# Reordered engine queues and a mix over two 64-row halves in a cross-attention, attention and gated-MLP kernel

## What is computed

```
x = x + xattn(layernorm(x), ctx)        # 16 heads of 32, 1601 context rows per batch, latent width 32
x = x + attn(layernorm(x))              # 32 query heads of 128, 8 key/value heads, 512 selected keys + 64 new ones
x = x + ffn(layernorm(x))               # silu(x W1) * (x W3) W2, inner width 1792
# W = base + mean(|w - base|) * sign(w - base) for each of W1, W2, W3
```

## Time and profile before

| | us |
|---|---|
| median of 3 runs (lowest, highest) | 922.68 (922.39, 923.87) |
| profiled execution, its own time | 919.89 |
| its span in the trace | 917.8 |
| PE busy in the span | 851.7 |
| cross-attention (trace, until the barrier) | to about 288 |
| attention with keys | about 288 to 796 |
| MLP | from about 796 |

### The profile page before, as it was taken

One profiled execution on the slowest core, in us unless ns is written; L12 is line 12 of the kernel. 1 busy time (PEld: TensorE's weight loads), 2 busy tenths in 40 slices (PEclk: granted clock), 3 DMA queues, 4 the chain that ended last, 5 costly groups with the idle time before them and its releaser, 6 DMA issues.

```text
span 917.8 us, 15508 instructions
## 1 busy us (share of the span) xinstructions
PE 851.7 (93%) x5338; PEld 650.9 (71%) x5338; DVE 603.3 (66%) x993; ACT 519.1 (57%) x1005; POOL 459.6 (50%) x294
## 2 busy tenths in 40 slices
PE   6898899888987889999999999999999999899998
PEld 4455455544433668888788887887878878788886
DVE  5965567555625268578486684776848759768884
ACT  5655546555554466386474774655746657555552
POOL 2698788786751054544444444345454454154430
PEclk9899999999999999999999999999999999999999
DMA  8654244104103515032050230501505002535531
GB/s 359 217 199 153 99 153 171 28 19 136 58 1 121 193 43 207 24 134 97 0 206 23 95 133 0 206 23 41 187 0 203 15 0 92 184 127 194 192 107 46
DMA packets 42338, 102.96 MB, mean 112 GB/s; under 512 B 7858, under 2 KB 12978, under 8 KB 41394
## 3 DMA queue, kind: packets, MB, share of 16 engines
q1 hardware_dynamic: 42002, 102.06, 31.7%
q10 hardware_dynamic: 288, 0.26, 0.1%
HBM read 96.95 MB, written 1.05 MB: 107 GB/s over the span
## 4 chain that ended last, share of the span: by engine, by line
PE 51%; POOL 5%; DVE 3%; issue 3%; ACT 2%; DMA 0%; SPq 0%; DVEq 0%; POOLq 0%; ACTq 0%
PE psum L1401 9%; PE psum L1382 9%; PE psum L1517 8%; PE psum L1413 5%; PE psum L1531 4%; POOL w_piece L1908 3%; PE psum L1440 3%; PE psum L1431 3%; PE psum L1455 3%; PE psum L1436 3%; ACT w_piece L1624 2%; PE psum L1422 1%; PE psum L1432 1%; PE psum L1434 1%; DVE probs_t_low L1742 1%
## 5 line engine op out<-in xcount | busy, mean ns | idle before, releaser
L1896 POOL TENSOR_TENSOR head_probs<-head_probs,inverse_den 128x576 f32<-128x576 f32 x128 | 147.5, 1153 | 203.7 <-DVE inverse_den L1749 203.7
L1003 DVE TENSOR_REDUCE max_part<-psum 128x1 f32<-128x804 f32 x128 | 121.2, 991 | 38.4 <-PE psum L698 38.0
L901 ACT ACTIVATE probs<-psum 128x512 f32<-128x512 f32 (+1 forms) x208 | 106.7, 608 | 47.4 <-PE psum L719 46.4
L1631 ACT ACTIVATE head_probs<-psum,neg_max 128x576 f32<-128x576 f32 x128 | 94.7, 740 | 46.2 <-DVE neg_max L1766 45.8
L1766 DVE TENSOR_REDUCE neg_max<-psum 128x1 f32<-128x576 f32 x128 | 96.9, 757 | 23.8 <-PE psum L1401 21.3
L567 POOL TENSOR_TENSOR prob_sums<-prob_sums,probs 128x1024 f32<-128x1024 f32 (+1 forms) x42 | 100.2, 2386 | 18.4 <-ACT probs L901 14.1
L1742 DVE TENSOR_TENSOR probs_t_low<-psum,probs_t_high 128x512 fp32r<-128x512 f32 x124 | 84.8, 684 | 16.6 <-ACT probs_t_high L1637 15.6
L1413 PE MATMUL psum<-ident,head_probs 128*128 128x128 f32 x496 | 78.7, 274 | 16.5 <-DVE probs_t_low L1742 15.1
L719 PE MATMUL psum<-q_t,c_t 97*128 97x512 f32 (+1 forms) x208 | 76.1, 445 | 14.2 <-ACT q_t L919 7.1
L1401 PE MATMUL psum<-k_high,query_t_high 128*128 (+1 forms) x256 | 86.5, 338 | 1.9 <-DVE query_t_low L1721 1.4
L567 POOL TENSOR_TENSOR prob_sums<-probs 128x1024 f32<-128x1024 f32 x30 | 71.3, 2380 | 23.9 <-ACT probs L901 23.8
(11 more groups left out here) (227 smaller groups left out, 1948.2 us busy)
## 6 DMA issues: line engine op xcount, KB each, us to landing
ctx_t_odd<-in_ctx_dram SPq DMA_DIRECT2D x4, 3202.0 KB, 11.0
ffn_raw<-in_L_ffn_w_dram SPq DMA_DIRECT2D x42, 256.0 KB, 3.9
ffn_raw<-in_L_ffn_mean_w_dram SPq DMA_DIRECT2D x42, 256.0 KB, 4.1
w_piece<-in_L_ffn_w_dram SPq DMA_DIRECT2D x21, 512.0 KB, 6.5
w_piece<-in_L_ffn_mean_w_dram SPq DMA_DIRECT2D x21, 512.0 KB, 7.5
cache<-in_ctx_dram SPq DMA_DIRECT2D x3, 3202.0 KB, 10.8
wq_nat<-in_L_attn_wq_dram SPq DMA_DIRECT2D x32, 256.0 KB, 7.4
wo_nat<-in_L_attn_wo_dram SPq DMA_DIRECT2D x32, 256.0 KB, 3.2
```

The lines of the kernel that those rows point to most:

```text
L901: act.activation(prob_buffer(b, t)[0:rows, half * BANK:(half + 1) * BANK], psum[0:rows, n % SCORE_BANKS, :], ACT.Exp, scale=XSCALE).then_i ...
L1003: dve.tensor_reduce(max_part[:, qt, pair:pair + 1], psum[:, bank:bank + 2, 0:PIECE_KEYS], AX.XY, ALU.max).then_inc(s_max, 1)
L1631: act.activation(probs[:, qt, :].rearrange("p (a k) -> p a k", a=2), psum[:, 2 * (qt % 2):2 * (qt % 2) + 2, 0:HALF], ACT.Exp, bias=neg_max ...
L1896: pool.tensor_tensor(probs[:, qt, :], probs[:, qt, :], rden[:, qt:qt + 1].to_broadcast([P, KEYS]), ALU.mult).then_inc(s["norm"], 1)
```

## The change

Nine edits, no change to what is computed:

- `mix`: the 64 rows of `u` and the 64 of denominators are no longer stacked. `u_all` is one copy of the whole bank of 128 partitions (L1025), `d_all` another (L926). The products take 64 contraction rows (half 0 rows 0 to 63, half 1 rows 64 to 127): 16 with 32 columns against `wv_u`, then 16 with one column against `den_of`.
- `wv_u` and `den_of` are set up by five small memsets and four transfers in place of three memsets and two transfers.
- `shift_row` copies two halves of 512; the turned maxima signal after four transposes and after eight; each half of the first scores waits for its half.
- `max_scores` 5 to 14 each stand one place earlier in PE's list, ahead of `values` where they stood behind it.
- For the batches 5, 6 and 7, `copy_den` follows the batch's exponentials; for 5 and 6 `tail_and_denominators` goes ahead of `turn_max`.
- ACT: `abs_sum` ahead of `output_weight_high(g, 0)`.
- DVE: `values_low` ahead of `add_output` of tile 0.

```diff
-    u_all = core.sb("u_all", [P, 2, BANK], ctx=own)
+    u_all = core.sb("u_all", [P, BANK], ctx=own)
+    d_all = core.sb("d_all", [P, BANK], ctx=own)
...
-            sp.wait_ge(s_zero, 2)
-            for base in (0, LKV):
-                sp.dma_start(wv_u[base:base + LKV, :, 0:XHD],
-                             arg["Wv_u"].rearrange("l (h d) -> l h d", h=XH)).then_inc(s_wv, 16)
+            for n in range(GROUPS):
+                heads = slice(n // 2 * XH // 2, (n // 2 + 1) * XH // 2)
+                sp.dma_start(wv_u[n * LKV:(n + 1) * LKV, :, :],
+                             arg["Wv_u"].rearrange("l (h d) -> l h d", h=XH)[:, heads, :]).then_inc(s_wv, 16)
...
-            pool.memset(wv_u[:, :, :], 0.0).then_inc(s_zero, 1)
+            pool.memset(den_of[:, :], 0.0).then_inc(s_zero, 1)
             pool.wait_ge(s_zero, 2)
-            for n, base in enumerate((2 * LKV, 3 * LKV)):
+            for n in range(GROUPS):
                 pool.wait_ge(s_mask, 3 + n)
-                pool.memset(wv_u[base:base + 1, :, XHD:XHD + 1], 1.0).then_inc(s_mask, 1)
+                pool.memset(den_of[n * LKV:n * LKV + 1, :], 1.0).then_inc(s_mask, 1)
...
-                mm.then_inc(s_mt, 1)
+                    if qt % 4 == 3:
+                        mm.then_inc(s_mt, 1)
...
-                    if t == 0 and half == 0:
-                        pe.wait_ge(s_shift, b + 1)
+                    if t == 0:
+                        pe.wait_ge(s_shift, 2 * b + half + 1)
...
                 for j in range(XH // 2):
                     for half in range(2):
-                        mm = pe.matmul(psum[half * SEQ:(half + 1) * SEQ, MIX_BANK, j * OW:(j + 1) * OW],
-                                       u_all[:, half, j * SEQ:(j + 1) * SEQ], wv_u[:, half * (XH // 2) + j, :],
-                                       start=True, stop=True)
+                        rows = slice(half * SEQ, (half + 1) * SEQ)
+                        pe.matmul(psum[rows, MIX_BANK, j * OW:j * OW + XHD], u_all[rows, j * SEQ:(j + 1) * SEQ],
+                                  wv_u[rows, j, :], start=True, stop=True)
+                for j in range(XH // 2):
+                    for half in range(2):
+                        rows = slice(half * SEQ, (half + 1) * SEQ)
+                        mm = pe.matmul(psum[rows, MIX_BANK, j * OW + XHD:(j + 1) * OW], d_all[rows, j * SEQ:(j + 1) * SEQ],
+                                       den_of[rows, :], start=True, stop=True)
                 mm.then_inc(s_o, 1)
...
                 maximum(4)
+                maximum(5)
                 values(b, range(0, 2))
                 for t in range(6, 10):
-                    maximum(t - 1)
+                    maximum(t)
                     scores(b, t)
-                maximum(9)
+                maximum(10)
                 values(b, range(2, 4))
                 for t in range(10, KT):
-                    maximum(t)
+                    maximum(t + 1)
                     scores(b, t)
-                maximum(KT)
+                maximum(KT + 1)
                 values(b, range(4, 6))
-                maximum(KT + 1)
                 maximum(KT + 2)
                 if b + 3 < BATCH:
                     compress(b + 3)
-                if lead:
                     turn_max(b + 1)
-                if b + 3 < BATCH:
                     natural(b + 3)
+                else:
+                    tail_and_denominators(b)
+                    if lead:
+                        turn_max(b + 1)
                 if lead:
                     scores(b + 1, 0)
                     scores(b + 1, 1)
-                tail_and_denominators(b)
+                if b + 3 < BATCH:
+                    tail_and_denominators(b)
...
-                act.wait_ge(s_mt, b + 1)
-                act.activation(q_t[SHIFT:STACK, b, :, :].rearrange("p (a h) n -> p a (h n)", a=2),
-                               psum[SHIFT:STACK, TURN_BANK:TURN_BANK + 2, :], ACT.Copy).then_inc(s_shift, 1)
+                for half in range(2):
+                    heads = slice(half * XH // 2, (half + 1) * XH // 2)
+                    act.wait_ge(s_mt, 2 * b + half + 1)
+                    act.activation(q_t[SHIFT:STACK, b, heads, :].rearrange("p h n -> p (h n)"),
+                                   psum[SHIFT:STACK, TURN_BANK + half, :], ACT.Copy).then_inc(s_shift, 1)
...
-                for half in range(2):
-                    act.activation(u_all[2 * LKV:P, half, :],
-                                   psum[half * 2 * LKV:(half + 1) * 2 * LKV, DEN_BANK, :],
-                                   ACT.Copy).then_inc(s_d, 1)
+                act.activation(d_all[:, :], psum[:, DEN_BANK, :], ACT.Copy).then_inc(s_d, 1)
...
-                    if t == 1 and b > 0:
+                    if t == 1 and 0 < b < BATCH - 2:
                         copy_den(b - 1)
...
                 if b + 3 < BATCH:
                     compressed(b + 3)
+                else:
+                    copy_den(b)
                 if b + 1 < BATCH:
                     shift_row(b + 1)
...
-                for half in range(2):
-                    dve.tensor_copy(u_all[0:2 * LKV, half, :],
-                                    psum[half * 2 * LKV:(half + 1) * 2 * LKV, U_BANK, :]).then_inc(s_u, 1)
+                dve.tensor_copy(u_all[:, :], psum[:, U_BANK, :]).then_inc(s_u, 1)
...
-                if this and i == 0:
-                    output_weight_high(g, i)
                 if last and i == 0:
                     for k in range(3):
                         abs_sum(g, k)
+                if this and i == 0:
+                    output_weight_high(g, i)
...
-                if i == 0 and last:
-                    add_output(g, 0, turn_bank(0))
                 if this and i == 0:
                     values_low(g)
                 if i == 0 and last:
-                    for qt in range(1, TT):
+                    for qt in range(TT):
                         add_output(g, qt, turn_bank(qt))
```

26 lines of the change are left out of this document (13 added, 13 removed).

## The result

The changed kernel takes **910.67 us** (median of four runs, 908.41 to 913.99) against 923.27 (922.39 to 924.50) for the kernel before: ratio **0.9865 [0.9826, 0.9905]**. It is faster, as forecast, but by 12.6 us where 23 were forecast, and above the range of 892 to 908. Its runs lie further apart than those of before; why, the clock will show. In this document times and ratios leave out runs more than 1.5% above the fastest of the same kernel, which happened to four of ten runs of split_mix alone.

The account below looks back on a forecast made before the run. PE, busy 93% of the span, was taken to bound the kernel, so orders win only where it waits. Terms -15.4 - 3.3 - 2.0 - 2.6 - 6.4 + 7.2 = -22.5 gave 900.0 us, range 892 to 908.

Parts of the forecast that it names:

- The attention's swaps: Attention: reordering ACT's sums and DVE's `values_low` removes PE's 2.2 us stall in each of groups 1 to 7: -15.4 us.
- Mix by halves: Cross-attention's mix: 64 instructions at 29 ns take 2.05 us, +0.9 in each of 8 mixes: +7.2 us.
- B: Rival: the mix's halves overlap, costing +0.2 or less, and the clock stays up in batches 5 and 6: 892.2; chance 0.20.
- C: Rival: the mix's row halves, writing one bank, take turns, 3.7 us per mix, +20.8 in all: 913.8; chance 0.06.
- D: Rival: each half of the mix waits out the other's whole latency, +13 us per mix: about 997; chance 0.02.
- three signs by which the prediction was to be known as wrong: Mix over 3 us or under 1.3; POOL's last add in batches 5/6 much later; ACT's last sum after output product.
- Maxima: Cross-attention, maxima one place earlier: 1.39 us less at `compress`, 0.7 more at first `values`; 0.65 in 5 batches: -3.3.
- Shift by halves: Shift row copied in halves, first half ready earlier: 0.3 us in five batches, 0.5 at the first turn: -2.0.
- Single copies: One copy each of values and denominators: 0.4 us in batches 1 to 5, 0.6 at last `copy_den`: -2.6.
- Batches 5 and 6: Sums ahead of the turn bring the mix earlier, despite a new 1.6 us wait on POOL: 3.2 us, twice: -6.4.
- 3.7 us before 232.35: With sums ahead of the turn, the four scores end at 228.7, 3.7 us before the next iteration's first maxima started.
- A: Rival: the cross-attention nets nothing, three-way pacing giving the moved maxima back; only the attention counts: 907.3; chance 0.14.

Follow-up runs that it names:

- split_mix: The changed kernel with the denominators' products moved ahead of the third tile's first maximum, before the rest of the mix: 911.25 us, ratio 0.9873.
- mix_only: The kernel before with only the new mix and its copies, no order changed: 941.46 us, ratio 1.0210.
- maxima_only: The kernel before with only the maxima moved one place earlier: 922.88 us, ratio 0.9996.
- maxima_tail: The kernel before with the maxima moved and the late order (sums ahead of the turn in batches 5 and 6): 921.14 us, ratio 0.9956.
- den_wide: The changed kernel with 31 streamed columns in each denominator product in place of one: 902.69 us, ratio 0.9783.
- u_products: The changed kernel without the denominators' products, a 33rd column of `wv_u` standing in for them: 893.09 us, ratio 0.9662.
- old_mix: The changed kernel with the mix, copies and `wv_u` of the kernel before: 899.48 us, ratio 0.9749.
- no_late: old_mix with batches 5 to 7 in the order of the kernel before: 898.98 us, ratio 0.9741.
- swaps_only: The kernel before with only the two swaps of the attention: 904.86 us, ratio 0.9808.
- ballast_31: old_mix with added 128-row products of 31 streamed columns each behind the mix, into unread columns: 907.50 us, ratio 0.9814.
- ballast_1: old_mix with added 128-row products of one streamed column each behind the mix, into unread columns: 909.71 us, ratio 0.9859.

## Why the prediction was wrong, step by step

- **The attention's swaps**: right. Forecast -15.4. Between the first and last query projections of these heads after needs 359.09 us, before 376.31: -17.2. Seven stalls of 2.2 are 15.4; most of the rest is one head that took 25.90 us before, 1.5 more than its like. Behind its stall, at 571, the clock fell (below). No kernel with the swaps has such a fall, and all four profiled without them (before, mix_only, maxima_only, maxima_tail) have one or two.
- **Mix by halves**: its length right, its consequence missed. Forecast +0.9 by the 29 ns step; measured 0.92 (den_wide 30.34 against u_products 29.42). Rivals B, C and D all fall with the 2.05 us of the mix: the halves neither overlap nor take turns. **This is where the prediction failed.** "The new one has 64... 64 x 29 + 0.2 = 2.05 us" priced the mix at its own length alone and "on the path" meant to it only what waits for its end. That the added products stream one column was used for their price and never asked as to the clock behind them. It had quoted the level of 0.50 in batch 5, but tied it to idle time and looked for it nowhere else. The fall costs 1.9 us in a steady batch (32.26 against 30.34). None of the three signs by which the prediction was to be known as wrong came true, since none of them looked at the clock; of what it listed to show it right, the 30.1 us between mixes is what missed.
- **Maxima**: forecast 0.65 a batch, measured 0.25. The gain at `compress` was near (1.16 for 1.39), the price at the first values was 0.90 and not 0.7: two terms with little between them.
- **Shift by halves**: forecast 0.3 a batch, measured 0.41 (30.29 in maxima_tail, 29.88 in old_mix).
- **Single copies**: forecast 0.4 a batch, measured 0.46 (u_products 29.42 against old_mix 29.88, with mixes of one length).
- **Batches 5 and 6**: forecast -6.4 for the order. Batches 5 to 7 together take 80.08 us before and 77.72 after; with three mixes at 0.9 and the 0.6 at the last `copy_den` the terms made it 80.08 - 6.4 + 2.7 - 0.6 = 75.8. Of the 1.9 missing, 0.7 is in batches 5 and 6 and 1.2 in batch 7, where the clock falls at 271. The step that failed here is what "3.7 us before 232.35" was put down to. From the end of the 16th maximum to the next iteration's first it is 9.6 us before, 6.2 after and 7.1 in no_late: the 3.4 us gained are near the 3.7 worked out, but 2.6 of them come with before's order too, from shorter waits and a clock that stays up; the order itself was worth 0.64 us in batch 5 and nothing in batch 6. The new wait on POOL is 0.36 us twice, not 1.6. POOL's last add ended where it was expected, 2.8 us behind the start of the 16th maximum; PE's own first rounds ended 2.5 us behind it and not 1.2.

The account of the profiled executions (forecast 897.4, measured 908.8, 11.4 apart): four steady batches 129.02 in place of 4 x 30.1, +8.6; batches 5 to 7 +1.9; up to the first mix +1.1 (84.75 against 83.66; swaps_only, unchanged there, has 86.89, so this is scatter as far as is known); from the last mix to the attention -0.3; the attention -1.8; from there to the end +1.0, unexplained (the fall at 905.8 stands behind PE's last product, which ends at 903.4). That makes 10.5. The other half of the argument is den_wide: the predicted kernel without the falls in the steady batches, at 902.69 us, lies 2.7 from the 900.0 forecast and inside its range.

Rivals A (907.3) and C (913.8) lie nearest to 910.67 by number, but neither mechanism is what happened: the mix took 2.05 us and not C's 3.7, and against A the cross-attention's other changes kept part of their gains (30.54 to 29.42 for a steady batch, without the added products).

**What stays open.** The exact condition of the fall isn't settled. The runs show it within 2 us of the reciprocal in 14 of 16 steady batches with 32 instructions of one column behind or between as many wider ones, in 2 of 4 with 8 columns, in none of 8 with 31; and not behind the mix of batch 4 in after. Nor do they show why batches 5 to 7 fall in den_wide and ballast_31, where no streamed column is missing, and in ballast_31 for longer than in ballast_1. So "31 columns keep the clock up" holds for the steady batches only. Whether a mix whose narrow products number 16 or fewer would keep the clock up wasn't tried.

## What to carry to other kernels

Price an added run of products twice: by its own length, and by the granted clock of what follows it, which was 1.9 us a batch here against 0.92 for the run itself. Where a product's pace doesn't change with its streamed columns, more of them are free; padding one column to 31 was worth some 8 us in this kernel (910.67 to 902.69), and not measurably anything on the ballast pair. Count the falls and read the mean clock beside the time: old_mix and the ballast pair were undecided by their times and decided by the clock. When a gain is measured against a stretch whose clock had fallen, find out first what made it fall: the time may come back by other means too, as it did in no_late, and then only once.

## What the runs showed of the hardware

- PE's clock fell to 1.2 GHz behind products of one streamed column with PE 100% busy by the trace (clock 0.67 at 117 us in after, busy share 1.00 from 115 on), at 64 rows as at 128. The Trainium skill (TensorE: Matmul & The Clock Gate, What's actually happening) ties the gate to how busy PE has been of late. The busy share of the records doesn't follow the clock here: it is 1.00 at this fall, and 0.83 at 214 us behind the mix of batch 4, where the clock stays at 1.00. A one-column product's record is 193 ns long and the next one starts 29 ns later, so the records overlap and the share can't show how little is streamed.
- A short stall can cost more than itself. Before has one of 2.06 us until 570.44, then this (columns as above):

```profile
570.00:571.00 1.00, 0.56 (x6) 1.00 0.00 0
571.00:572.00 1.00, 1.00 (x9) 0.86 0.00 0
572.00:573.00 1.00, 1.00 (x6) 0.50 0.00 0
...
575.00:576.00 1.00, 1.00 (x6) 0.94 0.00 0
```

The four traces without the swaps hold 28 such stalls and five such falls, each 1.1 to 1.5 us behind the end of one of these stalls (before 571.7, mix_only 651.3, maxima_only 516.4, maxima_tail 454.8 and 748.3), and the other 23 stalls have none. Why these five isn't shown.

- Products with 64 stationary columns follow each other every 29 ns, with 1, 8, 31, 32 or 33 streamed columns, with 64 rows or 128. With 32 stationary columns the step is 17.5 ns, though 65 are streamed. The halves of 64 rows gave no shorter step than the 128 rows. The Trainium skill (TensorEngine Tiling (Array Packing), Instruction Overhead) gives some 60 cycles for each product, an estimate of 25 ns at 2.4 GHz: close to the 29 here, above the 17.5 of `compress`'s tail with 32 stationary columns.
